# Two graph layers from one pass over an 8192 x 8192 adjacency: two buffers for the unpacked row, a ring of five chunks, x loaded behind the first row

## The reference

```python
# layer 0
deg = clip(sum(adj, axis=1) + 1, 1, None)
h_neigh = (adj @ X + X) / deg
out = relu(concat([X, h_neigh]) @ W + b)
out = out / max(norm(out, axis=1), 1e-12)
x = layernorm(x + out)
# layer 1
deg = sum(adj, axis=1)
neigh = adj @ x / (deg + 1)
x = layernorm(x + concat([x, neigh]) @ W1.T)
```

## Time and profile before

| | us |
|---|---|
| median of three runs | 761.63 |
| lowest and highest | 760.83, 764.16 |
| the profiled execution's own time | 762.74 |
| its span, from first to last instruction | 760.9 |
| TensorE busy | 630.8 (83%) |
| VectorE busy | 682.1 (90%) |
| ScalarE busy | 588.8 (77%) |
| GpSimd busy | 312.3 (41%) |

### The profile page before, as it was taken

How to read it: one execution, slowest core, us unless ns; L and a number is a source line. 1 busy time by engine, 2 the same in 40 slices (tenths; PEclk the granted TensorE clock), 3 DMA queues, 4 the chain that set the end, 5 groups by cost and what they waited for, 6 DMA issues and landing times.

```text
span 760.9 us, 27768 instructions
## 1 busy us (share of the span) xinstructions
PE 630.8 (83%) x11125; PEld 580.0 (76%) x11125; DVE 682.1 (90%) x2506; ACT 588.8 (77%) x815; POOL 312.3 (41%) x360
## 2 busy tenths in 40 slices
PE   1357687687777778979899998999999999998994
PEld 0246677676776677878788887989898989988994
DVE  4499998989998999899999999999999999987895
ACT  1978879989898888989889898888898888850021
POOL 0233323433421425664354545556553546341025
PEclk9987877989999997999999999999999999999998
DMA  9999999999999999999999999999999999900003
GB/s 361 406 366 402 420 347 420 422 420 418 421 419 419 419 419 407 382 419 419 419 414 420 408 421 402 420 413 408 413 391 420 399 418 394 420 24 2 2 18 102
DMA packets 41516, 274.54 MB, mean 361 GB/s; under 512 B 4455, under 2 KB 8615, under 8 KB 8615
## 3 DMA queue, kind: packets, MB, share of 16 engines
q1 hardware_dynamic: 39040, 270.55, 87.1%
q10 hardware_dynamic: 2342, 2.16, 0.9%
HBM read 270.60 MB, written 2.10 MB: 358 GB/s over the span
## 4 chain that ended last, share of the span: by engine, by line
PE 31%; DVE 25%; issue 13%; ACT 11%; DMA 11%; POOL 7%; ACTq 2%; DVEq 0%; POOLq 0%; SPq 0%
PE s_ps L385 17%; DMA a_in<-in_adj 11%; ACT junk L589 8%; DVE e L802 7%; DVE t_sb L809 6%; PE u_ps L404 5%; POOL small L1179 4%; PE p_ps L371 2%; PE z_ps L454 2%; DVE q_sb L870 2%; DVE y_sb L864 2%; ACTq L577 2%; PE p_ps L466 1%; DVE a_in L809 1%; POOL store L1211 1%
## 5 line engine op out<-in xcount | busy, mean ns | idle before, releaser
L589 ACT ACTIVATE junk<-a_in 128x2048 uint8<-128x2048 uint16 x256 | 488.4, 1913 | 8.8 <-DMA a_in<-in_adj 8.6
L385 PE MATMUL s_ps<-xh,t_sb 128*128 128x129 f16 x4096 | 388.2, 251 | 52.3 <-DVE t_sb L809 48.8
L385 PEld LDWEIGHTS s_ps<-xh,t_sb 128*128 128x128 fp8e4 x4096 | 314.7, 103 | 81.3 <-DVE t_sb L809 53.8
L802 DVE TENSOR_SCALAR e<-a_in 128x2048 uint8<-128x2048 f32 x256 | 314.1, 1234 | 18.7 <-DMA a_in<-in_adj 17.9
L1211 POOL COPY store<-pk 128x32 uint32<-128x32 uint32 (+1 forms) x250 | 176.1, 746 | 179.9 <-ACT pk L598 179.9
L809 DVE TENSOR_SCALAR t_sb<-pk 128x128 uint32<-128x128 uint32 x1024 | 159.1, 227 | 5.6 <-ACT pk L598 4.8
L371 PE MATMUL p_ps<-pow_h,e 128*128 128x16 f16 x2048 | 90.8, 171 | 65.7 <-DVE e L802 55.0
L371 PEld LDWEIGHTS p_ps<-pow_h,e 128*128 128x128 f16 x2048 | 77.6, 99 | 79.9 <-DVE e L802 60.1
L1179 POOL TENSOR_TENSOR small<-small,minus_half 128x4 f32<-128x4 f32 x32 | 68.8, 2150 | 151.8 <-DVE small L858 104.9
L404 PE MATMUL u_ps<-xh,u_sb 128*128 128x64 f16 x2976 | 105.6, 192 | 0.0
L404 PEld LDWEIGHTS u_ps<-xh,u_sb 128*128 128x128 fp8e4 x2976 | 100.6, 97 | 1.2
(11 more groups left out here) (119 smaller groups left out, 487.5 us busy)
## 6 DMA issues: line engine op xcount, KB each, us to landing
a_in<-in_adj SPq DMA_DIRECT2D x256, 1024.0 KB, 11.2
xl<-in_x ACTq DMA_DIRECT2D x4, 512.0 KB, 18.3
out_h<-e SPq DMA_DIRECT2D x8, 256.0 KB, 2.1
b_sb<-in_L_gnn_b ACTq DMA_DIRECT2D x3, 0.2 KB
w_sb<-in_L_gnn_W ACTq DMA_DIRECT2D x1, 32.0 KB
w_raw<-in_L_gnn_W ACTq DMA_DIRECT2D x1, 32.0 KB
```

The costliest lines, as they stand in the source:

```text
L385: last = nc.tensor.matmul(s_ps[:, n % 2, at:GW], t_sb[:, b // 2, b % 2::2], xh[:, b, at:GW], start=(b == 0), stop=False)
L589: nc.scalar.activation(junk[:, t % 2, :], halves[t % R], ACT.Copy, scale=1.0 / 128, accum_out=half_sum[:, n, c:c + 1]).then_inc(s_half, 1)
L802: nc.vector.tensor_scalar(e8[:, c, :], a_in[:, t % R, :], 1.0, float(CODE), ALU.is_equal, ALU.add).then_inc(s_e, 1)
```

## The change

- `t_sb` gets two buffers, row n in buffer n % 2; half h of row n may be unpacked when half h of row n - 2 is summed.
- The ring `a_in` has five slots, and so has the ring `v_sb` that lies over it in the tail.
- SP issues the four transfers of x behind the four chunks of row 0. ScalarE does one small copy at the start.
- On ScalarE and VectorE all four parts of x are split before the first chunk of row 1. VectorE prepares the bias behind chunk 1 of row 0, the weights behind row 1, and does the guards behind rows 20, 24, 28 and 32.
- Blocks with known G are no longer one matmul of 257 columns into 257, but G high (64 columns) and then G low, x high, x low and ones (193 columns), both starting at column 0 of the result, so that G's halves add up there. The first block of such a row has three: 64, 64, 129. `agg` has 193 columns.
- VectorE adds the halves of x's product in `mean`; GpSimd only keeps the degrees.

```diff
-R = 6
+R = 5
...
+GUARD = [20, 24, 28, 32]
...
-VR = 6
+VR = 5
...
-        t_sb = sb("t_sb", [P, NB // 2, 2 * P], FP8)
+        t_sb = sb("t_sb", [P, 2, NB // 2, 2 * P], FP8)
...
-        agg = sb("agg", [P, 2, BR, GW], F32)
+        agg = sb("agg", [P, 2, BR, SW], F32)
+        warm = sb("warm", [P, 1], F32)
...
                     sp.dma_start(a_in[:, t % R, :], adj_j[n // IL, n % IL, :, c * CH:(c + 1) * CH]).then_inc(s_in[t % R], 16)
+                if n == 0:
+                    for q in range(NC):
+                        sp.dma_start(x_in[:, q * CB:(q + 1) * CB, :].rearrange("p (j r) f -> p j (r f)", r=IL),
+                                     x_j[:, q * CB // IL:(q + 1) * CB // IL, :]).then_inc(s_x[q], 16)
...
-                    at = 0 if b < lows(n) else HP
-                    last = nc.tensor.matmul(s_ps[:, n % 2, at:GW], t_sb[:, b // 2, b % 2::2], xh[:, b, at:GW],
-                                            start=(b == 0), stop=False)
+                    row_bits = t_sb[:, n % 2, b // 2, b % 2::2]
+                    if b < lows(n):
+                        nc.tensor.matmul(s_ps[:, n % 2, 0:F], row_bits, g_hi[:, b, :], start=(b == 0), stop=False)
+                    if 0 < b < lows(n):
+                        last = nc.tensor.matmul(s_ps[:, n % 2, 0:SW], row_bits, xh[:, b, F:GW], start=False, stop=False)
+                        continue
+                    if b < lows(n):
+                        nc.tensor.matmul(s_ps[:, n % 2, 0:F], row_bits, g_lo[:, b, :], start=False, stop=False)
+                    last = nc.tensor.matmul(s_ps[:, n % 2, F:SW], row_bits, xh[:, b, HP:GW],
+                                            start=(b == 0 and not lows(n)), stop=False)
...
-            for q in range(NC):
-                act.dma_start(x_in[:, q * CB:(q + 1) * CB, :].rearrange("p (j r) f -> p j (r f)", r=IL),
-                              x_j[:, q * CB // IL:(q + 1) * CB // IL, :]).then_inc(s_x[q], 16)
+            act.wait_ge(s_const, 1)
+            nc.scalar.copy(warm[:, :], ident[:, 0:1])
...
             def bias():
 
+                dve.wait_ge(s_w, 80)
...
-                if n:
-                    dve.wait_ge(s_sum, (n - 1) * 2 + h + 1)
+                if n >= 2:
+                    dve.wait_ge(s_sum, (n - 2) * 2 + h + 1)
...
-                dve.wait_ge(s_xsum, e + 1)
+                hi, lo = (agg[:, par, :, F + i * F:2 * F + i * F] for i in range(2))
+                link(nc.vector.tensor_tensor(hi, hi, lo, ALU.add))
...
+                if n == 1:
+                    for q in range(NC):
+                        split_x(q)
                 compare(n, 0)
...
                 if n == 1:
-                    split_x(3)
-                if n == 2:
                     weights()
-                    bias()
-                if 3 <= n < 7:
-                    guard_x(n - 3)
+                if n in GUARD:
+                    guard_x(GUARD.index(n))
...
-            def join_x(e):
+            def keep_degrees(e):
 
                 pool.wait_ge(s_agg, (e + 1) * BR)
-                hi, lo = (agg[:, e % 2, :, HP + i * F:HP + (i + 1) * F] for i in range(2))
-                nc.gpsimd.tensor_tensor(hi, hi, lo, ALU.add).then_inc(s_xsum, 1)
```

More of the change, by code:

```diff
@@ L34 @@
 GW = HP + XW
+SW = F + XW
 PK = P // 8
@@ L383, in sum_quarter @@
                 for b in range(i * CB, (i + 1) * CB):
[L384 to L386 removed]
+                    row_bits = t_sb[:, n % 2, b // 2, b % 2::2]
[8 more added lines that the diff above has]
+                                            start=(b == 0 and not lows(n)), stop=False)
                 if i == 3:
[L388 removed]
+                    last = nc.tensor.matmul(s_ps[:, n % 2, F:SW], id8[:, :], xh[:, n, HP:GW],
                                             start=False, stop=True)
@@ L607, in take_sums @@
                     act.wait_ge(s_dcol, e - 1)
-                at = 0 if lows(n) else HP
-                nc.scalar.copy(agg[:, e % 2, k, at:GW], s_ps[:, n % 2, at:GW]).then_inc(s_agg, 1)
+                at = 0 if lows(n) else F
+                nc.scalar.copy(agg[:, e % 2, k, at:SW], s_ps[:, n % 2, at:SW]).then_inc(s_agg, 1)
             def take_cat(e):
@@ L897, in begin_acc @@
                 par = e % 2
-                known = [k for k in range(BR) if lows(e * BR + k)]
-                if known:
-                    dve.wait_ge(s_dcol, e + 1)
                 for k in range(BR):
                     n = e * BR + k
-                    if k in known:
+                    if lows(n):
                         ins = nc.vector.scalar_tensor_tensor(out=acc[:, n, :], in0=z_ps[:, k, F:2 * F],
-                                                             scalar=agg[:, par, k, 2 * HP:GW], in1=agg[:, par, k, 0:F],
+                                                             scalar=agg[:, par, k, SW - 1:SW], in1=agg[:, par, k, 0:F],
                                                              op0=ALU.mult, op1=ALU.add)
                     else:
-                        ins = nc.vector.tensor_scalar(acc[:, n, :], z_ps[:, k, F:2 * F], agg[:, par, k, 2 * HP:GW], None,
+                        ins = nc.vector.tensor_scalar(acc[:, n, :], z_ps[:, k, F:2 * F], agg[:, par, k, SW - 1:SW], None,
                                                       ALU.mult)
@@ L988, in _ @@
                 e, k = n // BR - 1, n % BR
+                if n == 1:
+                    for q in range(NC):
+                        split_x(q)
                 compare(n, 0)
-                if n == 1:
-                    split_x(0)
                 if n:
@@ L998, in _ @@
                 compare(n, 1)
-                if n == 1:
-                    split_x(1)
+                if n == 0:
+                    bias()
                 if n >= START[1]:
@@ L1180, in root @@
                                         ALU.pow).then_inc(s_root, 1)
-            def join_x(e):
+            def keep_degrees(e):
                 pool.wait_ge(s_agg, (e + 1) * BR)
-                hi, lo = (agg[:, e % 2, :, HP + i * F:HP + (i + 1) * F] for i in range(2))
-                nc.gpsimd.tensor_tensor(hi, hi, lo, ALU.add).then_inc(s_xsum, 1)
-            def join_g(e):
-                known = [k for k in range(BR) if lows(e * BR + k)]
-                if known:
-                    hi, lo = (agg[:, e % 2, known[0]:BR, i * F:(i + 1) * F] for i in range(2))
-                    nc.gpsimd.tensor_tensor(hi, hi, lo, ALU.add)
                 nc.gpsimd.tensor_copy(dcol[:, e * BR:(e + 1) * BR],
-                                      agg[:, e % 2, :, 2 * HP:GW].rearrange("p k o -> p (k o)")).then_inc(s_dcol, 1)
+                                      agg[:, e % 2, :, SW - 1:SW].rearrange("p k o -> p (k o)")).then_inc(s_dcol, 1)
             def own_rows(e):
@@ L1236, in _ @@
                 e, k = n // BR - 1, n % BR
-                if e >= 0 and k == 1:
-                    join_x(e)
                 if e >= 0 and k == 2:
```

27 lines of the change are left out of this document (7 added, 20 removed).

## The result

The change makes the kernel slower: 770.87 us median (769.78 to 775.98) against 762.59 us for the kernel before on the same chip; ratio 1.0122, 95% interval 1.0071 to 1.0174. The profiled execution is the one of 770.86 us, span 769.0; it stands against the 760.9 us span of before.

What follows compares the result with a forecast made beforehand. It took the start as below full DMA rate, the middle as DMA-bound, the last rows as DMA and TensorE about equally. Terms -6.5 and +1.6 sum to -4.9 us, forecast 756.7 us (chance 0.62), range 752 to 766.

Steps and rivals of the forecast that it cites:

- Start, -6.5 us: First 120 us: x behind the first row and moved preparations let the DMA hold 420 GB/s; -6.5 us, bounds -7.1 and -1.
- The guards at rows 20, 24, 28 and 32 ... 0 us: Rows 20 to 32: 2.4 us each on VectorE, covered by some 7 us; 0 us, 9.7 together without cover.
- G join, +1.6 us: Rows 46 to 63: 842 more matmuls at 2.5 ns, 2.1 us, a quarter in a gap; +1.6 us, bounds 0 and +21.
- rival 2: Split blocks of rows 46 to 63: second load not hidden, TensorE waits; at +25 ns 21 us, 776 us; chance 0.10.
- DMA and TensorE are equally close to being the bound: Last rows: 40.0 us for the bytes against a 41.28 us period, so work added on TensorE counts.
- Rival 4: Late split blocks: weight loads do not overlap each other, a pair takes 206 ns; 79 us, 834 in all; chance 0.02.
- Rival 1: Start stays bound by the engines, 2 to 3 us won, less 1.6; about 760.5 us, no change; chance 0.21.
- Ring of five, 0 us: Adjacency ring: issue to landing falls from 11.8 to 9.3 us, least 5.5; 0 us, bounds 0 and 32 us.
- rival 3: Groups from row 12 on: ring of five runs dry, 2.5 us lost each, up to 32 us, 787; chance 0.05.
- Two buffers, 0: Unpacked row: VectorE waited only 0.7 us for TensorE before unpacking; 0 us, at best -0.7.
- POOL's joins, 0: Group ends: POOL's joins go, VectorE adds x's halves, 0.43 us per group; 0 us, bounds -1 and +2.5.
- The warning sign it named: Prediction wrong if the start gains 6 us without an earlier end: late rows then bound by TensorE and VectorE before 480 us.

Runs made afterwards that it cites:

- e10: Kernel before with x behind the first row and moved preparations, guards of x in rows 4, 6, 8 and 10: 758.52 us, 0.9952 of before.
- e9: Kernel before with x behind the first row and moved preparations, guards in rows 20, 24, 28 and 32, run a second time: 760.42 us, 0.9975 of before.
- e1: Kernel before with only x behind the first row and the moved preparations, guards in rows 20, 24, 28 and 32: 761.19 us, 0.9978 of before.
- e4: Kernel before with the whole change except the G join (new start, ring of five, two unpacked-row buffers): 761.06 us, 0.9973 of before.
- e3: Kernel before with only the ring of five and two buffers for the unpacked row: 764.71 us, 1.0028 of before.
- e12: Kernel before with only the ring of five, one buffer for the unpacked row: 764.54 us, 1.0025 of before.
- e2: Kernel before with only G's halves joined by PE (64 + 193 columns), x's halves added by VectorE: 773.05 us, 1.0152 of before.
- e5: Kernel before with every known block's matmul split into 64 and 193 columns, no halves joined by PE: 770.07 us, 1.0098 of before.

## Why the prediction was wrong

It gave 756.7 us and a range of 752 to 766; 770.87 is outside it. By its steps:

- **Start, -6.5 us: right in the place, too large in what is kept.** The stretches, ScalarE's first chunk and, in e10, the end came as forecast (ScalarE sums the last chunk from 670.30 us on, before from 675.40). But "The guards at rows 20, 24, 28 and 32 ... 0 us" was wrong: about 1.9 us (e9 against e10), and the median keeps 2 us of the start's 6, 4 with early guards. The cover of 7 us was that of the ring; TensorE had none, and waited 2.05 us in row 20. Nor was the move of the guards needed for the gain, as the term had it.
- **G join, +1.6 us: this step failed.** Its price is +10 to +12. Its first part is a mis-sized term: the second matmul of a 64 and 193 pair costs 4.4 ns, not 2.5, which over 842 blocks is 3.7 us and not 2.1. The second, larger part has no line in the prediction: 6.2 us of "issue" from 480 us on and 3.3 before, from instructions that come late. I priced a matmul by the columns and by its load, and took the rate of 64-column matmuls from the tail, where the DMA is idle. The number was right there (3.84 us for 128 in the changed kernel's tail as well) and did not carry to rows in which the DMA is full. The upper bound of the term, +21 us, did hold the loss; the range was cut at the mild forms of rival 2.
- **"DMA and TensorE are equally close to being the bound": wrong.** With half of the bytes the period stays 41.28 us. 40.0 us for the bytes against 41.28 was in the prediction; it should have been read as 1.3 us of slack on the DMA and none on TensorE, so that each block's loss there counts in full. The 0.72 us gap covered little.
- **Rival 2** had place and number of blocks right and the mechanism wrong: the load of the 193-column matmul is hidden (117 ns for an even cut as well). Rival 4 is out: the pair takes 116.3 ns with two loads of 128 columns, so loads do overlap matmuls. Rival 1 is out by the stretches.
- **Ring of five, 0 us, and rival 3:** +2.0 us alone, 0 behind the new start (e1 against e4). The landing times came about as computed: a median of 9.1 us from 120 to 480 us (9.3 computed), and late 8.3 with a least of 5.0, which is where rival 3 was to begin. It did not: in e3 and e4 the late period is the old 41.28 us. In e3 only the start of the late rows comes later (chunk 180 at 480.32 us, before at 478.83).
- **Two buffers, 0:** right (e12 against e3). **POOL's joins, 0:** the join alone costs some 3 us more than the split alone (+10.1 and +7.2 us in the medians, on two chips), intervals overlapping, so this is not settled.
- **The warning sign it named** came, "the start gains its 6 us and the end does not come earlier", but not for the reason given with it (late rows that were bound before 480 us already): with the start part alone the end does come earlier (chunk 255 at 669.89 us in e1), and the change loses it again, 2.9 us between chunks 99 and 180 and 10.8 us behind them. Behind 480 us the join is the part that does it. In the middle it is more likely the guards and the clock, as in e4: of their leads e2 and e5 lose 0.4 us and nothing between the same two chunks. This was not parted further.
- **Readings of the rows that were off** and moved no term: the granted clock is 1.00 in the first two stretches of the earlier trace rows, not below full in all; and of the last slices of the earlier trace rows the very last has 102 GB/s.

The sum by parts: start -2.0, the ring behind it 0, the G join +10 to +12, together +8 to +10 us; measured +8.3 (ratio 1.0122, +9.3 us by it).

The version that beats both is e10: the start part, ring of six, one `t_sb`, joins on POOL, and the guards of x in rows 4, 6, 8 and 10: 758.52 us, 0.9952 of before.

## What to carry to other kernels

A matmul more on the engine that sets the period has three prices: its columns, here some 5 ns of its own, and its instructions, which come over the same DMA as the data. The third was nothing while the DMA had room (202 GB/s), and with a DMA at 380 to 420 GB/s it was the largest. Take a rate of short matmuls from a stretch whose DMA is as full as where you want to use it. And before calling two resources equally close to the bound, halve the load of one: 20 rows with half the bytes settled in one run what the rows could not.

## What was not expected of the hardware

- TensorE waits up to 1.8 us at a time for its own instructions ("issue") when it starts some 20 matmuls per us, each with its load, beside a DMA of 375 to 400 GB/s; beside 202 GB/s it starts 21 per us and does not wait. The Trainium skill (Runtime: NRT & Kernel Launch, Instruction fetch mechanics) says that the stream is refilled in blocks of 16 KiB by DMA of the engine's own, and that this is hidden by the pace at which instructions are issued. The sizes agree (1.67 MB in 102 packets); the rest does not hold here, 6.2 us in 195 us were not hidden. Beside the full DMA a packet starts 2.4 us later than beside the half-loaded one, and TensorE resumes 1.2 to 1.6 us behind its end. How many blocks are ahead, and when one is asked for, no run here shows.
- A wait on a semaphore long reached is not free for TensorE: 1,611 instructions with waits cost 10.1 us beside a full DMA. From row 45 on they cost 8.2 us beside the full and 3.6 us beside the half-loaded one.
- A second matmul costs 4.4 to 5.4 ns beyond its columns. The Trainium skill (TensorE: Matmul & The Clock Gate, Wait — 56ns, not 53.3ns?) has 2.5 ns for each; an estimate by it would be 842 x 2.5 = 2.1 us where the rows give 3.7.
- Half of the adjacency's bytes in the last 20 rows changed nothing: 0.9995 of before.
